# Convolution and attention outputs made channel-major: mixing weights and R held still in TensorE, bias and x added on VectorE, tokens transposed for the layer norms

## The reference, cut to what matters

```python
# block 1, a mixture of four small experts on the normalised image, plus x
t1 = x + conv(groupnorm(x))       # hidden = relu(w1 @ xn + b1), 4 x 96 = 384 rows; y = w2 @ hidden + b2, weighted
# block 2, linear attention on tokens (a token: the 96 channels of one position), plus t1
t2 = t1 + attn(layernorm(t1))     # per image A = fk^T fv (96 x 96), masked; out = (q @ A) @ proj_w + proj_b
# then
out = t2 + ffn(layernorm(t2))     # two binarised layers 96 -> 384 -> 96, each quantised by group maxima over 6 images
```

## Time and profile before

| what | value |
|---|---|
| median of 3 runs | 851.54 us (850.2 to 852.54) |
| the profiled execution | 856.85 us, of it 855.0 us from first to last instruction |
| busy: PE, DVE, ACT, POOL | 809.4, 632.5, 461.7, 181.0 us |
| mean TensorE clock granted | 0.969 of full speed |
| instructions | 17997 |
| memory traffic | 29.51 MB read, 18.67 MB written |

### The profile page before, as it was taken

How to read it: one execution, slowest core, us unless ns; L and a number is a source line. 1 busy time by engine, 2 the same in 40 slices (tenths; PEclk the granted TensorE clock), 3 DMA queues, 4 the chain that set the end, 5 groups by cost and what they waited for, 6 DMA issues and landing times.

```text
span 855.0 us, 17997 instructions
## 1 busy us (share of the span) xinstructions
PE 809.4 (95%) x6053; PEld 624.7 (73%) x6053; DVE 632.5 (74%) x1977; ACT 461.7 (54%) x654; POOL 181.0 (21%) x216
## 2 busy tenths in 40 slices
PE   6888999999999999999999999999999799999991
PEld 3456688888888888888888888888888655555550
DVE  3585477777776777777677777777777257999997
ACT  2453354454454445445444544544443299988981
POOL 1460222223223222322322232232232000000000
PEclk8899899999999999999999999999999599999997
DMA  9950001111000001100000110000010010563433
GB/s 214 213 118 16 15 30 30 30 29 56 28 28 28 28 28 33 52 28 28 28 28 28 41 43 28 28 28 28 28 42 14 15 43 0 150 196 105 142 113 113
DMA packets 19979, 48.69 MB, mean 57 GB/s; under 512 B 4561, under 2 KB 4847, under 8 KB 19951
## 3 DMA queue, kind: packets, MB, share of 16 engines
q1 hardware_dynamic: 19552, 47.72, 20.1%
q10 hardware_dynamic: 399, 0.60, 0.2%
HBM read 29.51 MB, written 18.67 MB: 56 GB/s over the span
## 4 chain that ended last, share of the span: by engine, by line
PE 86%; DVE 4%; SPq 3%; ACT 3%; issue 2%; POOL 1%; DMA 1%; DVEq 0%; ACTq 0%; POOLq 0%
PE slot L1007 18%; PE slot L988 11%; PE slot L856 10%; PE slot L1053 9%; PE slot L1017 6%; PE slot L1014 6%; PE slot L1172 5%; PE slot L1143 5%; PE slot L1204 4%; PE slot L1208 4%; PE slot L1002 3%; SPq L443 2%; DMA big<-in_x 1%; PE slot L920 1%; ACT big L822 1%
## 5 line engine op out<-in xcount | busy, mean ns | idle before, releaser
L1007 PE MATMUL slot<-w2s,hT 128*112 128x96 f32 x1344 | 162.7, 269 | 0.0
L1421 DVE TENSOR_SCALAR xh<-t,ln_mv,ln_rs 112x96 f32<-112x96 f32 x434 | 109.2, 323 | 60.0 <-POOL ln_rs L605 60.0
L1007 PEld LDWEIGHTS slot<-w2s,hT 128*112 128x112 f32 x1344 | 141.6, 177 | 10.7
L748 ACT ACTIVATE hT<-slot,b1c,w_unit 128x784 f32<-128x784 f32 x96 | 95.9, 1004 | 90.8 <-PE slot L988 90.8
L755 ACT ACTIVATE stage<-slot,minus_one 112x768 f32<-112x768 f32 x64 | 52.5, 821 | 119.0 <-PE slot L1053 118.9
L579 POOL TENSOR_TENSOR xn_lo<-xn,xn_hi 96x784 f16<-96x784 f32 x32 | 53.4, 1669 | 245.0 <-ACT xn_hi L737 245.0
L605 POOL TENSOR_TENSOR ln_rs<-ln_ve,pow_half 112x7 f32<-112x7 f32 x62 | 91.8, 1481 | 4.8
L1014 PE MATMUL slot<-big,W1b 99*128 (+1 forms) x360 | 90.5, 332 | 0.1
L1017 PE MATMUL slot<-big,W1b 96*128 (+1 forms) x360 | 90.2, 332 | 0.0
L1427 DVE TENSOR_REDUCE ymax<-slot 128x784 f32 (+1 forms) x90 | 83.9, 960 | 6.4 <-PE slot L1017 5.9
L1053 PE MATMUL slot<-qkvw,xh1T 97*112 97x192 f32 x448 | 86.4, 335 | 0.9 <-ACT xh1T L769 0.9
(11 more groups left out here) (194 smaller groups left out, 1363.4 us busy)
## 6 DMA issues: line engine op xcount, KB each, us to landing
out<-t2T SPq DMA_DIRECT2D x56, 294.0 KB, 3.1
xs<-in_x SPq DMA_DIRECT2D x32, 294.0 KB, 3.1
big<-in_x SPq DMA_DIRECT2D x7, 1176.0 KB, 15.8
xs<-out SPq DMA_DIRECT2D x24, 294.0 KB, 3.3
big<-out SPq DMA_DIRECT2D x1, 1764.0 KB, 11.2
out<-big SPq DMA_DIRECT2D x6, 294.0 KB, 2.6
big<-in_x SPq DMA_DIRECT2D x2, 588.0 KB, 25.0
con<-shape_consts ACTq DMA_DIRECT2D x1, 445.5 KB, 6.3
```

The lines of the kernel that those rows point to most:

```text
L748: nc.scalar.activation(hT[:, t, :].rearrange("p (a n) -> p a n", a=2), halves((0, one, 2)[t], P), ACT.Relu, scale=w1_unit[:, t:t + 1], bia ...
L1007: ins = mm(o[:, j, :], hT[:, t, j * TOK:(j + 1) * TOK], w2s[:, v, t, :], start=False, stop=t == TILES - 1, skip_group_check=True)
L1421: ins = V.tensor_scalar(dst[:, j, :], src[:, j, :], ln_mv[n][:, j, 0:1], ln_rs[n][:, j:j + 1], ALU.subtract, ALU.mult)
```

## The change

The mixing and the last product of attention swap their operands: `w2s` and `R` stand still, and 392 columns of hidden values or normalised tokens move. Both results come out channel-major. The transposes of x into the mixing group and the bias matmul go. VectorE adds the bias (a column per channel) and x in the one instruction that makes `t1cm` (channel-major), and adds `t1cm` and the attention output straight into `t2T`, which SP stores. For the layer norms two new calls of `to_tokens` (7 transposes each) and two new copies on ScalarE (`tok1`, `tok2`) bring t1 and t2 token-major; the norms are applied in place. The `to_channels` of t2 and ScalarE's copy of it go. Statistics and application of the second norm move from the end of step i-1 to the start of step i. The biases of the experts are loaded as `b2c`, 96 x 4, in one transfer of single elements in place of three of rows, and GpSimd's splitting of them goes.

```diff
             def mix(v, k, t):
+                for h in range(2):
+                    ins = mm(S[k][0:C, h, 0:HALF], w2s[:, v, t, :], hT[:, t, h * HALF:(h + 1) * HALF],
+                             start=t == 0, stop=t == TILES - 1, skip_group_check=True)
...
+            def to_tokens(k, src, done):
+                for j in range(CHUNKS):
+                    ins = tr(flat(k)[0:TOK, j * P:j * P + C], src[:, j * TOK:(j + 1) * TOK], start=j % CH_A == 0)
+                ins.then_inc(done, 1)
...
-                    for j in range(CHUNKS):
-                        ins = mm(flat(one)[0:TOK, j * P:j * P + C], xh1T[:, j * TOK:(j + 1) * TOK], R[:, :],
+                    for h in range(2):
+                        ins = mm(S[3][0:C, h, 0:HALF], R[:, :], xh1T[:, h * HALF:(h + 1) * HALF],
                                  start=True, stop=True, skip_group_check=True)
                     ins.then_inc(ao_ready, 1)
...
+            def tokens(dst, k, done):
+                nc.scalar.copy(dst[:, :, :], chunks(k, CHUNKS, P, C)).then_inc(done, 1)
...
+                        V.scalar_tensor_tensor(t1cm[r][:, :].rearrange("p (a n) -> p a n", a=2), halves(1, C),
+                                               bias2[:, 1:2], xs[r][:, :].rearrange("p (a n) -> p a n", a=2),
+                                               ALU.add, ALU.add).then_inc(t1_ready, 1)
...
-            for n in range(PARTS):
-                load(b2r[n * E:(n + 1) * E, :], b2)
+            load(b2c[:, :], b2.rearrange("e o -> o e"))
```

More of the change, by code:

```diff
@@ L251, in build @@
         ln_rs = [sb(f"ln_rs{n}", [TOK, CHUNKS]) for n in range(2)]
-        xh1 = sb("xh1", [TOK, CHUNKS, C])
-        xh2 = sb("xh2", [TOK, CHUNKS, C])
+        w0_image = sb("w0_image", [TOK, CHUNKS])
+        tok1 = sb("tok1", [TOK, CHUNKS, C])
+        tok2 = sb("tok2", [TOK, CHUNKS, C])
         xh1T = sb("xh1T", [C + 1, HW])
@@ L765, in step @@
                     relu(1, 1)
+                if ffn:
+                    act.wait_ge(tok2_in_psum, i - 1)
+                    tokens(tok2, 3, tok2_ready)
+                if experts and not between:
                     relu(2, 2)
@@ L769, in step @@
                     nc.scalar.copy(*channels(xh1T[0:C, :], 0)).then_inc(xh1T_ready, 1)
[L770 to L779, removed]
+                    exp_kv(0, 3, 0, CH_A)
                 if experts and next_:
                     norm_image(m + r, 1 - r, i + 1)
+                if attend:
+                    exp_kv(1, 0, CH_A, CHUNKS - CH_A)
+                if ffn:
+                    wait_apart(act, x2p_ready, i - 1, act_passed)
+                    nc.scalar.copy(*channels(big[0:C, i - 2, 0, :], 2)).then_inc(hi_ready, 1)
+                if experts:
+                    act.wait_ge(tok1_in_psum, i + 1)
+                    tokens(tok1, 1, tok1_ready)
                 if between:
@@ L1082, in step @@
                     hidden(0, 0, r)
+                    pe.wait_ge(tok1_ready, i)
                     wait_count(pe, ymax_done, 3 * (i - 3) + 2)
[L1084 to L1087, removed]
+                    hidden(1, 1, r)
+                if ffn:
+                    pe.wait_ge(t2_ready, i - 1)
+                    to_tokens(3, t2T[r], tok2_in_psum)
+                if experts and not first:
                     wait_count(pe, ymax_done, 3 * (i - 3) + 3)
                     hidden(2, 2, r)
-                    pe.wait_ge(h_ready, 3 * i + 1)
                 def x1_to_channels():
@@ L1094, in x1_to_channels @@
                         pe.wait_ge(ymax_done, 3 * QIMAGES)
-                    to_channels(0, xh1, x1T_ready)
+                    to_channels(0, tok1, x1T_ready)
+                if experts and not first:
+                    pe.wait_ge(h_ready, 3 * i + 1)
                 if attend and not second:
@@ L1506, in step @@
                 if experts:
-                    stats(0, t1[r], 1 if isinstance(i, int) and i == 0 else 2 * i, CH_A)
-                if out_ and ffn:
-                    for t, k in ((0, 0), (2, other), (1, 2)):
-                        absmax(f, t, k)
-                if experts:
-                    apply(0, t1[r], xh1, i, xh1_ready)
+                    dve.wait_ge(tok1_ready, i + 1)
+                    stats(0, tok1, 1 if isinstance(i, int) and i == 0 else 2 * i)
+                if ffn:
+                    for t in range(TILES):
+                        absmax(f, t, t)
                 if attend:
                     dve.wait_ge(ao_ready, i)
-                    V.tensor_tensor(t2[:, :, :], t1[1 - r][:, :, :], chunks(one, CHUNKS, P, C),
+                    wait_count(dve, t2T_stored[1 - r], 16 * (m + r - 1))
+                    V.tensor_tensor(t2T[1 - r][:, :].rearrange("p (a n) -> p a n", a=2), halves(3, C),
+                                    t1cm[1 - r][:, :].rearrange("p (a n) -> p a n", a=2),
                                     ALU.add).then_inc(t2_ready, 1)
-                if attend and not (isinstance(i, int) and i - 1 >= QIMAGES):
-                    dve.wait_ge(t2_ready, i)
-                    stats(1, t2, 2 * i + 1)
-                    apply(1, t2, xh2, a, xh2_ready)
+                if experts:
+                    apply(0, tok1, tok1, i, xh1_ready)
             for i in range(FIRST):
-                step(i // 2, i % 2, attend=i >= 1, out_=i >= 2)
+                step(i // 2, i % 2, attend=i >= 1, ffn=i >= 2)
                 if i == 1:
```

275 lines of the change are left out of this document (130 added, 145 removed).

## The result

The changed kernel takes 903.93 us, the median of 4 runs (900.9 to 907.3). The kernel before takes 851.19 beside it. The ratio is 1.0619, with a 95% interval of 1.0573 to 1.0666. So it is 6.2% slower, where 824 us was forecast.

A forecast was written before the change was run, and what follows sets the result against it. The prediction took TensorE to bound the kernel: 30 steps falling from 18.69 to 17.82 us give 26.1, plus 1.4 at the ends, 27.5 us, so the median falls from 851.54 to 824 us, range 808 to 839.

The forecast's parts named there:

- GpSimd has slack: Main loop step: GpSimd's power would end a us before the second norm's application begins.
- move ahead of the second exponential, and ScalarE is free again at 10.0: Main loop step: the next image's high and low norm copies go earlier, with ScalarE free before kv ends.
- The rival of a longer VectorE chain: Main loop: VectorE's instructions and hand-offs take longer than priced, 18.2 to 18.6 us a step, 835 to 849 us; chance 0.15.
- The slow rival: Main loop: short TensorE idles bring the clock to 1.2 GHz in every second step, costing 45 us, 869 us; chance 0.06.
- a stretch of 6% idle at 1.00: From 720 to 760 us TensorE idles 2.34 of 40 us at full clock; cited against the slow rival.
- TensorE's work: Main loop step: 8.25 us removed and 6.55 added, so TensorE's step falls by 1.70 us to 16.99.
- the step that I walked through: One main loop step from its first hidden matmul: 16.99 us of TensorE work plus waits, 17.8 us.
- The transposes of xh2 with the wait for t1cm: Main loop step, after the second kv piece: forecast as 0.67 us plus a wait of 0.23.
- the low part: Main loop step: the first FFN tile waits for xh2's low part after A, 0.35 us with the hand-off.
- the 27.5 forecast: Whole kernel: 26.1 us gained over 30 loop steps plus 1.4 us at the ends.
- The forecast of -1.4 for the drain: After the loop: a longer wait at step 32 against 2.5 us and 0.3 of R saved, net -1.4 us.
- the prediction's reading that the stall was the queue's and not the load's: Start of the kernel: loading b2c costs +1 us, with +7 as the far bound, since the full queue stalls.

The follow-up runs named there:

- experiment 3: The changed kernel with seven unused matmuls of 512 columns ahead of TensorE's wait for xh2 in each step: 881.84 us.
- experiment 5: Experiment 2 plus one unused GpSimd sum of two SBUF operands, 96 x 384, per step beside the second norm's application: 849.55 us.
- Experiment 2: The changed kernel with ScalarE's norm of the next image moved from before the second exponential to behind the copy of tok1: 834.46 us.
- experiment 7: Experiment 2 with the load of b2c issued by ScalarE's queue in place of SyncE's: 832.36 us.
- experiments 4 to 6: One unused GpSimd instruction per step: a sum in the kernel before, 855.17 us; the same sum in Experiment 2, 849.55; a copy in the kernel before, 857.74.
- experiment 9: The kernel before with filler matmuls in the last step alone, 11 ahead of the transposes of xh1 and 6 ahead of A: 851.64 us, ratio 0.9974.
- experiment 4: The kernel before with one unused GpSimd sum of two SBUF operands, 96 x 384, per step behind the second norm's power: 855.17 us.

## Why the prediction was wrong

**The step that failed** is the sentence "GpSimd has slack", with the one behind it: the copies of the next image's norm "move ahead of the second exponential, and ScalarE is free again at 10.0". I asked whether GpSimd and ScalarE would be late. They weren't. I didn't ask what GpSimd's instruction would then run beside. The move put its subtraction of 1.67 us on top of the second norm's application. There one of the application's instructions waits for most of the subtraction (3.27 us for 1.76), and VectorE's chain had no slack left, by my own account. The rival of a longer VectorE chain went to 18.6 us a step; the hold alone makes it 19.4 (experiment 3).

The Trainium skill has this rule in "SBUF — State Buffer", section "Who interferes with whom": VectorE's copies and tensor_scalar in their two-port modes share an SBUF port pair with GpSimd, and whoever starts first keeps it for the whole instruction, while the other stands still. The traces agree: a TENSOR_SCALAR of SBUF operands was held (1.84 us for 0.32), and t1cm, which reads PSUM, was not (1.02 beside the subtraction). The hold falls short of GpSimd's instruction by 0.16 to 0.34 us. That the port is the mechanism is the page's word, and no run here shows which mode VectorE was in; the runs show that VectorE stands still. It was there to be read before the prediction.

**The clock.** The slow rival had the right mechanism, an idle in the step that brings TensorE to 1.2 GHz, at a chance of 0.06. I rejected it with a stretch of 6% idle at 1.00. That sum of small idles says little of one long one. The changed kernel has one idle of 1.40 to 1.56 us in each step; its clock was 1.00 from 110 to 210 us even so, and 0.91 to 0.93 in the middle of the loop. With the idle filled (experiment 3) or cut to 0.56 (experiment 5) the middle of the loop has 1.00. The price was 22 us, and not 45, since each event costs 1.0 us, about one slow A, and not 3: 20.5 us a step from the A at 236.06 on, against the 19.44 of experiment 3. The Trainium skill's rule that I had cited there ("TensorE: Matmul & The Clock Gate", on psum-queue depth-cycling: small idles between groups make the clock swing) was nearer to what happened than the row that I set against it, though the idle here is a wait and not a cycling through PSUM.

**TensorE's work was right.** Mixing 3.96 us (forecast 3.96), R 1.31 (1.32), transposes of t1cm 0.66 (0.62), of t2T 0.58. Experiment 2 has the step that I walked through, 17.90 for 17.82. The second kv piece with its wait takes 1.18 (415.86 to 417.04), as forecast. The transposes of xh2 with the wait for t1cm take 0.94, where 0.67 and 0.23 were forecast. The largest miss is the low part: A with the wait behind it takes 1.81 (400.67 to 402.48), where 1.19 and 0.35 were forecast.

**The ends.** In experiment 2's profile against that of before, the stretch up to the A of step 2 is shorter by 1.8 us (forecast 0), the 28 steps by 20.8 (521.93 less 501.16), the last two steps are longer by 1.0, and what follows the last A is shorter by 2.4. The sum is 24.0, for the 27.5 forecast; by medians the gain is 19.7. The loop is short by 3.6 of it: 0.74 a step in place of 0.87, since the new step is 0.08 longer than forecast and the old one was taken as 18.69, one step of the trace, where the mean is 18.64. The forecast of -1.4 for the drain was not met. The last two figures together are 1.4 shorter, but they include one more step of the loop (17.64 for 18.58), so the drain alone is 0.5 shorter. The start can't be read from one profile: in experiment 7, with the same loop, it is 0.1 us shorter than before and not 1.8.

So the 903.93 is: 834.5 for the change without the overlap, 47 for the hold, 22 for the clock.

## What to carry to other kernels

When a change moves an instruction on an engine with slack, ask what it will now run beside, and not only whether it is in time. On the path, a long GpSimd instruction on SBUF must not lie beside VectorE's tensor_scalar of SBUF operands. Beside t1cm, which reads PSUM, it cost nothing here. That VectorE's copies within SBUF can be held too is what the Trainium skill says ("SBUF — State Buffer", "Who interferes with whom"); no run here has one beside a long GpSimd instruction on the path. In the trace this shows as a row that is longer than its twins, with no wait in front of it: compare the max of a group with its median. And a tight hand-off chain makes such a stall expensive twice, since TensorE's idle then takes its clock too; a few filler matmuls tell the two costs apart.

## What was not expected of the hardware

- The hold is shorter than GpSimd's instruction by 0.15 to 0.35 us (experiments 4 to 6 and the changed kernel), and GpSimd's own row is hardly lengthened: 1.67 us in most steps of the changed kernel, and 1.74 in its first ones, where the application takes 3.11 to 3.12. VectorE's instruction already under way may end first; that wasn't tested by itself.
- Not every VectorE instruction on SBUF is held. In the kernel before the subtraction (416.09 to 417.76) lies on three statistics of t1, which read SBUF; no statistics instruction of that kernel is longer than 264 ns, with a median of 243.
- Seventeen to twenty-three filler matmuls in the last step alone move the whole time: 7 us with the new order (832.36 to 825.42), 2 us with the old (experiment 9).
- A load of 384 single elements, which had looked dangerous for the start, took 5.23 us of issue in place of the 5.64 of the loads that it replaced. When it left SyncE's queue, the next load stood there for 6.69 us in its stead (experiment 7). This fits the prediction's reading that the stall was the queue's and not the load's.
- The clock doesn't follow from one idle's length alone. In TensorE's timeline of the changed kernel, the same wait of 1.40 us leaves A at full clock in one step and not in the next:

```profile
194.59 0.88 PE L858 MATMUL slot<-con,tok 112*96 112x112 f32 x7 [1.40 <-DVE tok L1427]
196.20 1.43 PE L1149 MATMUL slot<-stage 112*96 112x96 f32 x14
...
214.05 0.88 PE L858 MATMUL slot<-con,tok 112*96 112x112 f32 x7 [1.40 <-DVE tok L1427]
215.65 2.40 PE L1149 MATMUL slot<-stage 112*96 112x96 f32 x14
```

From 110 to 210 us the clock is 1.00, from there to the A at 687.08 every step has a slow one. The drain of the kernel before does the same from one execution to another: with the same idle of 2.26 us ahead of it, its kv takes 4.82 us in its own profile, where the mean clock from 660 to 680 us is 0.64, and 2.53 us in that of experiment 4, where it is 1.00. What decides between them stays open, and no run was made for it.
